# Adding the FFN's first bias on TensorE instead of ScalarE, and rectifying 512 columns at once

## The reference, cut to what matters

```
x_q  = fake_quant(layernorm(x), s1, -8, 7)
b1_q = fake_quant(b1, s1 * sw1, INT32_MIN, INT32_MAX)      # round(b1 / (s1*sw1)) * (s1*sw1)
h    = x_q @ W1_q.T + b1_q                                 # 256 -> 1024
h_q  = fake_quant(relu(h), s2, 0, 15)
out  = h_q @ W2_q.T + b2_q                                 # 1024 -> 256
```

## Time and profile before

| | |
|---|---|
| median of 3 runs | 298.29 us (298.26 to 298.51) |
| span of the profiled execution | 296.1 us |
| PE busy | 250.3 us (85% of the span) |
| DVE busy | 223.3 us (75%) |
| ACT busy | 202.2 us (68%) |
| POOL busy | 128.1 us (43%) |
| ACT `h_i` (L636), 128 operations | 48.3 us |

### The profile page before, as it was taken

The page is one execution under the profiler, slowest core; times in us unless marked ns, Lnnn a source line. Parts: engine busy times, 40 slices in busy tenths (PEclk is TensorE's granted clock), DMA queues, the critical chain, the costliest instruction groups (busy, mean ns, idle before and its releaser), DMA issues.

```text
span 296.1 us, 8723 instructions
## 1 busy us (share of the span) xinstructions
PE 250.3 (85%) x2816; PEld 183.8 (62%) x2816; DVE 223.3 (75%) x570; ACT 202.2 (68%) x444; POOL 128.1 (43%) x266
## 2 busy tenths in 40 slices
PE   0056227899999999999999999999999999999653
PEld 0045126867767777777777777777777767665441
DVE  2977418797887979797979797979888877784441
ACT  3213025667679787878787878888887978679423
POOL 7625039444471717263635454445453451520110
PEclk9999557799999999999999999999999999999875
DMA  7921101252111113121211121112112111200101
GB/s 165 340 92 45 35 0 38 62 167 49 37 48 45 45 45 83 41 52 41 80 45 45 40 80 43 45 51 68 44 38 72 41 38 41 72 3 4 35 0 38
DMA packets 31786, 17.41 MB, mean 59 GB/s; under 512 B 6544, under 2 KB 31376, under 8 KB 31760
## 3 DMA queue, kind: packets, MB, share of 16 engines
q1 hardware_dynamic: 29696, 17.06, 21.8%
q10 hardware_dynamic: 2064, 0.02, 0.4%
HBM read 6.31 MB, written 2.10 MB: 28 GB/s over the span
## 4 chain that ended last, share of the span: by engine, by line
PE 69%; issue 11%; DVE 10%; POOL 5%; ACT 4%; DMA 1%; ACTq 0%; POOLq 0%; DVEq 0%
PE ps_misc L972 34%; PE ps_av L972 13%; PE ps_max L972 12%; PE ps_exp L972 9%; DVE turns L697 2%; ACT h_i L636 2%; DVE xn L867 1%; DMA q_diag<-mxT 1%; POOL rot L475 1%; DVE by_cos L796 1%; POOL q_rows L441 1%; DVE by_sin L801 1%; DVE xn L772 1%; POOL k_rows L442 1%; POOL rstd L515 1%
## 5 line engine op out<-in xcount | busy, mean ns | idle before, releaser
L810 DVE TENSOR_REDUCE mx<-ps_max 128x4 f32<-128x512 f32 x128 | 87.3, 686 | 30.0 <-PE ps_max L972 26.9
L607 ACT ACTIVATE expo<-ps_exp 128x512 f32<-128x512 f32 x128 | 77.7, 607 | 19.6 <-PE ps_exp L972 18.1
L972 PE MATMUL ps_exp<-q_diag,k_stack 128*128 128x512 f32 x128 | 60.3, 471 | 0.4 <-DMA q_diag<-mxT 0.4
L972 PE MATMUL ps_av<-expo,v_strip 128*32 128x128 f32 x1024 | 54.1, 285 | 0.0
L972 PE MATMUL ps_max<-k_stack,q_diag 96*128 96x128 bf16 (+1 forms) x512 | 52.9, 226 | 0.8 <-DVE mx L810 0.8
L636 ACT ACTIVATE h_i<-ps_misc,b1q,relu_scale 128x128 int16<-128x128 f32 x128 | 48.3, 470 | 2.5 <-PE ps_misc L972 2.5
L972 PEld LDWEIGHTS ps_max<-k_stack,q_diag 96*128 96x128 bf16 (+1 forms) x512 | 30.8, 99 | 24.5 <-issue 23.3
L500 POOL TENSOR_TENSOR v_strip<-v_comp,zeros 128x32 f32<-128x32 f32 x128 | 28.0, 256 | 19.4 <-PE ps_av L972 19.4
L972 PEld LDWEIGHTS ps_av<-expo,v_strip 128*32 128x32 f32 x1024 | 20.3, 108 | 21.8 <-issue 14.7
L483 POOL TENSOR_TENSOR q_rows<-rot,q_rows 128x256 f32<-128x256 f32 x16 | 11.6, 725 | 36.0 <-ACT q_rows L582 36.0
L972 PEld LDWEIGHTS ps_exp<-q_diag,k_stack 128*128 128x128 f32 x128 | 24.4, 190 | 1.5 <-issue 0.8
(11 more groups left out here) (122 smaller groups left out, 514.3 us busy)
## 6 DMA issues: line engine op xcount, KB each, us to landing
q_diag<-q_comp SPq DMA_DIRECT2D x128, 64.0 KB, 2.0
w<-in_L_ffn_W_dram SPq DMA_DIRECT2D x2, 1024.0 KB, 8.2
out_dram<-y SPq DMA_DIRECT2D x8, 256.0 KB, 2.2
c_in<-in_ctx_dram SPq DMA_DIRECT2D x16, 64.0 KB, 2.1
x_all<-in_x_dram SPq DMA_DIRECT2D x1, 1024.0 KB, 5.8
x_all<-in_x_dram SPq DMA_DIRECT2D x1, 512.0 KB, 4.7
q_diag<-mxT SPq DMA_DIRECT2D x32, 8.0 KB, 1.8
x_all<-in_x_dram SPq DMA_DIRECT2D x2, 128.0 KB, 2.6
```

Of the source, the lines that this page charges most:

```text
L607: act.activation(expo[:, g % EXPO, :], ps_exp[g % 2][:, :], ACT.Exp, scale=SCALE).then_inc(exp_done, 1)
L810: dve.tensor_reduce(out=mx[:, r, 4 * g:4 * g + 4], in_=ps_max[g % 2][:, :].rearrange("p (h k) -> p h k", h=4), axis=AX.X, op=ALU.max).then ...
L972: return pe.matmul(out, lhsT, rhs, start=start, stop=stop, skip_group_check=True, **kw)
```

## The change

Two operations take the place of four per half. PE first writes the bias into the whole bank by one more product, 128 x 512, and the eight products of the half accumulate on it. Its weights are `b1_rows` (72 partitions x 128): the rounded b1, an integer, split into three bf16 parts whose sum is exact, at rows 0 to 7, 32 to 39 and 64 to 71, one row per block of 128 channels. The moving side is `b1_pick` (72 x 8 x 128), which holds ones where the row's block is the column's block. ACT then rectifies the half with one operation of 128 x 512 that keeps its scale from a pointer and has no bias.

What comes with it: b1 is loaded as 8 partitions x 128. POOL clears `b1_rows` and `b1_pick` in step 1, ahead of `v_strip`. ACT writes the ones into `b1_pick` by three copies in step 3 at g = 1. `round_b1` on DVE becomes eight operations on 8 x 128, six of them each waiting for the one before. PE waits once, at its first half, for both. `h_i` and `hq` now lie in the memory of the raw `w1`, which is not read any more by then.

```
@@ fill_strips (POOL, step 1)
+                pool.memset(b1_rows[:, :], 0.0).then_inc(b1_cleared, 1)
+                pool.memset(b1_pick[:, :, :], 0.0).then_inc(b1_cleared, 1)
+                pool.wait_ge(b1_cleared, 2)
                 pool.memset(v_strip[:, :, :, :], 0.0).then_inc(strips_ready, 1)
@@ relu (ACT)
-                for c in range(4):
-                    f = 4 * half + c
-                    ins = act.activation(h_i[:, r, f, :], ps_misc[PIECE_BANK[(H0, H1)[half]]][:, 128 * c:128 * c + 128],
-                                         ACT.Relu, bias=b1q[:, f:f + 1], scale=relu_scale[:, :])
-                ins.then_inc(relu_done, 1)
+                act.activation(h_i[:, r, 4 * half:4 * half + 4, :],
+                               ps_misc[PIECE_BANK[(H0, H1)[half]]][:, :].rearrange("p (f t) -> p f t", f=4),
+                               ACT.Relu, scale=relu_scale[:, :]).then_inc(relu_done, 1)
@@ body (ACT)
+                    if g == 1 and not st.looped and st.s == 3:
+                        act.wait_ge(b1_cleared, 2)
+                        for part in range(3):
+                            ones = bcast(ident[0:FC, 0:FC], 2, 128)
+                            act.copy(b1_pick[32 * part:32 * part + FC, :, :], ones).then_inc(b1_picked, 1)
@@ round_b1 (DVE)
-                link(dve.tensor_scalar(b1i[:, :], b1[:, :], r_h_scale[:, 0:1], None, ALU.mult), wprep)
-                dve.tensor_scalar(b1q[:, :], b1i[:, :], relu_scale[:, :], None, ALU.mult).then_inc(bias_ready, 1)
+                dve.wait_ge(b1_cleared, 2)
+                link(dve.tensor_scalar(b1i[:, :], b1[:, :], r_h_scale[0:FC, 0:1], None, ALU.mult), wprep)
+                link(dve.tensor_copy(b1f[:, 0, :], b1i[:, :]), wprep)
+                link(dve.tensor_copy(b1_rows[0:FC, :], b1f[:, 0, :]), wprep)
...
+                dve.tensor_copy(b1_rows[32:32 + FC, :], b1m[:, :])
+                dve.tensor_copy(b1_rows[64:64 + FC, :], b1f[:, 0, :]).then_inc(bias_ready, 1)
@@ hidden (PE)
+                if not st.looped and st.s == S_FFN and half == 0:
+                    pe.wait_ge(bias_ready, 2)
+                    pe.wait_ge(b1_picked, 3)
                 st.wait(pe, xqT_ready, S_FFN, 1, 1)
+                picked = b1_pick[:, 4 * half:4 * half + 4, :].rearrange("p f t -> p (f t)")
+                mm(ps[:, :], b1_rows[:, :], picked, True, False)
                 for f in range(4):
                     for c in range(DC):
                         ins = mm(ps[:, 128 * f:128 * f + 128], w1T[:, c, 4 * half + f, :],
-                                 xqT[:, r, 128 * c:128 * c + 128], c == 0, c == DC - 1)
+                                 xqT[:, r, 128 * c:128 * c + 128], False, c == DC - 1)
```

More of the change, by code:

```diff
@@ L22 @@
 QMIN, QMAX, HMAX = -8.0, 7.0, 15.0
+B1_ROWS = 2 * 32 + FC
 ROPE_FREQ = float(np.float32(10000.0) ** np.float32(-0.5))
@@ L161, in xattn_ffn_kernel @@
         b2q = sb("b2q", [128, DIM])
-        b1 = sb("b1", [128, FC])
-        b1i = sb("b1i", [128, FC], I32)
-        b1q = sb("b1q", [128, FC])
+        b1 = sb("b1", [FC, 128])
+        b1i = sb("b1i", [FC, 128], I32)
+        b1f = sb("b1f", [FC, 2, 128])
+        b1m = sb("b1m", [FC, 128], BF16)
+        b1_rows = sb("b1_rows", [B1_ROWS, 128], BF16)
+        b1_pick = sb("b1_pick", [B1_ROWS, FC, 128], BF16)
         w1 = sb("w1", [128, FC, DIM])
         w2 = sb("w2", [128, DC, FFN])
+        w_flat = [w1[:, :, :].rearrange("p c d -> p (c d)"), w2[:, :, :].rearrange("p c f -> p (c f)")]
         w_i = [sb("w1_i", [128, 2048], I16), sb("w2_i", [128, 2048], I16)]
@@ L228, in xattn_ffn_kernel @@
         xqT = sb("xqT", [128, 2, DIM], BF16)
-        h_i = sb("h_i", [128, 2, FC, 128], I16)
-        hq = sb("hq", [128, 2, FC, 128], BF16)
+        h_i = w_flat[0][:, 0:1024].bitcast(I16).rearrange("p (r f t) -> p r f t", r=2, f=FC)
+        hq = w_flat[0][:, 1024:2048].bitcast(BF16).rearrange("p (r f t) -> p r f t", r=2, f=FC)
         x2_b = sb("x2_b", [128, 2, DIM])
@@ L258, in xattn_ffn_kernel @@
         bias_ready = sem("bias_ready")
+        b1_cleared = sem("b1_cleared")
+        b1_picked = sem("b1_picked")
         wmax_ready = sem("wmax_ready")
@@ L330, in copy_wT @@
             copy(dst, src).then_inc(wT_ready[n % 2], 1)
-        w_flat = [w1[:, :, :].rearrange("p c d -> p (c d)"), w2[:, :, :].rearrange("p c f -> p (c f)")]
         out_pairs = out_d.rearrange("(k two) t d -> k t two d", two=2)
@@ L415, in _ @@
                 (wout[:, :, :], wout_d.rearrange("(c p) d -> p c d", p=128)),
-                (b1[:, :], b1_d.rearrange("(c p) -> p c", p=128)),
+                (b1[:, :], b1_d.rearrange("(c p) -> c p", p=128)),
                 (bout[:, :], all_rows(bout_d)),
@@ L631, in relu @@
                 st.wait(act, hq_ready, S_FFN, 2, half - 3)
-                if not st.looped and st.s == S_FFN and half == 0:
-                    act.wait_ge(bias_ready, 2)
-                for c in range(4):
-                    f = 4 * half + c
-                    ins = act.activation(h_i[:, r, f, :], ps_misc[PIECE_BANK[(H0, H1)[half]]][:, 128 * c:128 * c + 128],
-                                         ACT.Relu, bias=b1q[:, f:f + 1], scale=relu_scale[:, :])
-                ins.then_inc(relu_done, 1)
+                act.activation(h_i[:, r, 4 * half:4 * half + 4, :],
+                               ps_misc[PIECE_BANK[(H0, H1)[half]]][:, :].rearrange("p (f t) -> p f t", f=4),
+                               ACT.Relu, scale=relu_scale[:, :]).then_inc(relu_done, 1)
             def body(st):
@@ L748, in round_b1 @@
             def round_b1():
-                link(dve.tensor_scalar(b1i[:, :], b1[:, :], r_h_scale[:, 0:1], None, ALU.mult), wprep)
-                dve.tensor_scalar(b1q[:, :], b1i[:, :], relu_scale[:, :], None, ALU.mult).then_inc(bias_ready, 1)
+                dve.wait_ge(b1_cleared, 2)
+                link(dve.tensor_scalar(b1i[:, :], b1[:, :], r_h_scale[0:FC, 0:1], None, ALU.mult), wprep)
+                link(dve.tensor_copy(b1f[:, 0, :], b1i[:, :]), wprep)
+                link(dve.tensor_copy(b1_rows[0:FC, :], b1f[:, 0, :]), wprep)
+                link(dve.tensor_tensor(b1f[:, 1, :], b1f[:, 0, :], b1_rows[0:FC, :], ALU.subtract), wprep)
+                link(dve.tensor_copy(b1m[:, :], b1f[:, 1, :]), wprep)
+                link(dve.tensor_tensor(b1f[:, 0, :], b1f[:, 1, :], b1m[:, :], ALU.subtract), wprep)
+                dve.tensor_copy(b1_rows[32:32 + FC, :], b1m[:, :])
+                dve.tensor_copy(b1_rows[64:64 + FC, :], b1f[:, 0, :]).then_inc(bias_ready, 1)
             def norm1_stats(st):
```

## The result

The changed kernel takes 304.38 us, the median of 4 runs (303.50 to 305.47), against 298.40 us for the kernel before, the median of 4 runs (298.26 to 300.06). The ratio is 1.0199, with a 95% interval of 1.0157 to 1.0241: slower by 2.0%, clear of noise. The prediction had 303.5 us in a range of 301.0 to 305.2.

The account below looks back on a forecast made before the run. PE was taken to bound steps 6 to 18. Product 5.7, last steps -0.9 and filling +0.4 gave +5.2 us: span 296.1 to 301.3, median 298.29 to 303.5, range 301.0 to 305.2.

Parts of the forecast that it names:

- The bound and the product: Steps 6 to 18: PE sets the pace, nothing hides the added products, 13 x 2 x 0.22 = 5.7 us.
- Rival A: Steps 6 to 18: the product is half hidden and costs 0.13 us, so +2.9, 301.2 us; chance 0.09.
- The rectifier: ACT, each half: one operation of 0.70 us replaces four of 1.50 together; worth time only in the last three steps.
- The last steps: Steps 19 to 21: shorter rectifier less added products gives -0.9 us, ends -0.3 and -2.7.
- Step 20: Second-to-last step: sooner rectified first half less the late second half, together -0.22 us at the half clock.
- Its first term: Step 20, up to PE's transposes: product in front and short rectifier, 0.22 - 0.80 = -0.58 us.
- The second: Step 20, second half: its added product takes 0.43 us at the half clock, of which about 0.36 stick out.
- the branch with the full clock: Step 20: if PE's clock stays full because the gap before it shrinks, the step gives -1.4 us.
- Rival C: From 268 us on: all PE gaps go and the clock stays full, 7.2 us gained, 298.1 us; chance 0.03.
- The filling steps: Before step 6: POOL's clears cost 0.4 us; ACT's copies, DVE's chain, b1's DMA and moved buffers cost 0.
- rival B: Steps 4 and 5: DVE's chain delays maxima and their DMA, PE's clock falls; +7.4, 305.7 us; chance 0.07.
- a first full step over 1 us late: Start of the first full step: beginning over 1 us late would show the forecast wrong and point to rival B.

Follow-up runs that it names:

- one rectifier alone: Kernel before with one 128 x 512 rectifier per half, the bias left out, no product and no preparation; 295.01 us, ratio 0.9889.
- no product: Changed kernel without the bias product, so b1 is left out of the result; preparation and single rectifier stay; 295.97 us, ratio 0.9933.
- two products: Changed kernel with the bias product issued twice per half, the second writing the same values again; 310.06 us, ratio 1.038.
- the end on DVE: Kernel before with the first half in bank 2 from step 18, and DVE doing ACT's four operations per half in steps 20 and 21; 298.40 us.
- another bank: Kernel before with the first half of the hidden layer in bank 2 from step 18 on, no operation changed; 296.28 us, ratio 0.9931.
- the preparation alone: Changed kernel's whole preparation in its places, but four rectifiers per half with raw b1 as bias and no product; 299.88 us, ratio 1.0043.
- the chain spread: Changed kernel with DVE's eight `round_b1` operations one per group in step 5 instead of in a row in step 4; 304.17 us, ratio 1.0167.
- the end alone in another bank: Kernel before, with early-issued product and single rectifier only in steps 20 and 21, first half in bank 2 from step 18, preparation moved earlier; 294.98 us.
- the version prepared late: As the end alone in another bank, but clears in step 16, DVE's rounding in step 17, ACT's copies in steps 17 to 19; 296.88 us.

## Why the prediction was right, point by point

**The bound and the product: right.** The prediction read PE as busy throughout in steps 6 to 18 and priced 26 products at 0.22 us, 5.7. The trace shows 5.78, and the steps of 14.45, 14.89 and 15.325 us with none, one and two products show that nothing hides any part of it. Rival A (a half hidden) is out. The Trainium skill, "TensorE: Matmul & The Clock Gate", section "Back-to-back issue gap", gives about 131 ns for a product of 512 columns in a sustained stream and 216 for an isolated one. In this busy stream it was 220, which agrees with the second figure and not with the first; the measurement decides.

**The rectifier: right in size.** Chosen 0.70 us, measured 0.687. That it is worth nothing where PE doesn't wait for it is shown by the kernel with one rectifier alone. The Trainium skill, "ScalarE: Activation LUTs", section "What ACT_TABLE_LOAD costs", gives 706 ns by its formula; the trace has 687, within 3% of it.

**The last steps: mechanism right, one term mis-sized.** Predicted -0.9, in the trace -2.16. Step 19 (-0.04 predicted, -0.11 measured) and step 21 (-0.5, -0.43) came out. Step 20 gave -1.62 where the sum had -0.22. Its first term was right: from the start of the half to the transposes it is 1.61 us instead of 2.20, -0.59 where the prediction had -0.58. The second was not: from there to the next first half it is 6.82 instead of 7.85, -1.03 where the prediction had +0.36 at the half clock. The clock was full there, and the branch with the full clock (-1.4 for the step) is what came. Rival C needed the full clock in step 21 as well, and there it was half.

That a shorter gap brings the full clock is likely, but no rule. Over the 3.1 us from the transposes of step 20 on, the mean clock is 0.50 and 0.63 in the two traces with the gap of 1.60 us. With the gap of 0.78 it is 1.00 in six traces, but 0.54 and 0.52 in those of no product and two products. With a gap of 0.37 it is 1.00 for the end on DVE and 0.51 for another bank.

**The filling steps: mis-sized the other way.** Predicted +0.4, in the trace +1.88, by the medians of the preparation alone +1.2. What failed is the step from POOL's clears to the maxima. Their own part, 0.45 at `rstd`, was as predicted (0.4), but the issue time ahead of the maxima is no constant: 5.59 to 5.93 us in the five kernels that clear nothing in the filling steps, 5.62 to 6.41 in the nine that do. In the trace of the preparation alone `rstd` is 0.48 us late (27.09), the maxima 0.88, step 6 0.56. For the DVE chain, which I then suspected, the run with the chain spread shows no gain. ACT's copies were not run by themselves. The first trace has PE waiting 0.97 us for ACT's `q_comp` at 52.00, behind them, but the transpose that waited 1.47 for DVE at 52.43 comes at 53.52, 1.09 late, no more than the maxima. How the rest divides stays open.

By its own sign, a first full step over 1 us late, the forecast had to yield to rival B in the first trace. What B said is not in it: PE has no wait for the DMA in step 4 there, and the clock is full from 60 us on. In the second execution of the changed kernel even the sign is absent. But B's picture does occur. The two latest starts of step 6, 91.77 (no product) and 90.20 (chain spread), follow waits for that DMA of 1.63 and 1.20 us, behind which the mean clock is 0.50 and 0.70 up to 70 us. Behind one of 1.47 (the end alone in another bank) it stayed at 1.00. Over all traces step 6 begins at 87.18 to 88.01 us in the five kernels without clears in the filling steps, at 87.42 to 91.77 in the six that clear in step 1, and at 88.46 to 89.30 in the three that clear in step 0.

**The sum.** +5.2 predicted; +5.5 in the trace, as 5.78 + 1.88 - 2.16; +4.7 to +6.0 by medians. Two errors, of about 1.3 in the end and of 0.8 to 1.5 in the filling, had opposite signs and nearly cancelled. That the total was good to 1 us was partly luck.

## What to carry to other kernels

Moving work to relieve an engine costs its full price on the engine that sets the pace, and gains only where that engine waits: here 13 steps paid 0.44 us each for a gain that the last steps alone could use. Do such a thing only in those steps, and first ask whether the wait can be removed without any operation, by giving the piece another buffer. Before placing preparation on an engine that is idle half of the time, look at what stands directly behind it: if that is the head of a chain, its idle time hides little. And look at what the other engines run beside it.

## What the runs showed of the hardware

- POOL's fill is priced by the element of a partition, not by the byte: 1024 bf16 columns took 0.94 us, 2048 f32 columns 1.81, 4096 int32 columns 3.51.
- DVE and POOL do not meet at semaphores alone. An operation of DVE of 128 x 64 (`turns`), which waits for nothing of POOL's, took 4.65 us instead of 0.20 and ended 0.06 us behind POOL's fill of `q_diag`; with 1.0 us more of fills behind that it took 5.68. Other operations of DVE ran beside fills at their usual length, such as `wmax` over 2048 columns, 2.27 us beside the fills of step 1 (at 24.05 in the changed kernel) and 2.28 with none beside it (at 20.45).
- A wait of PE can be paid twice. In the version prepared late a wait of 2.06 us was followed by a step at a mean granted clock of 0.90 that took 13.32 instead of 12.21 us. At the end, a gap of 0.78 instead of 1.60 was followed by the full clock in six traces and by about half of it in two, so a single trace doesn't settle what a gap costs.
- The clock in the filling steps and the issue time ahead of the shared maxima change from one execution to the next: the same 17 us at 0.50 in one and at 1.00 in another, 6.36 against 5.76 us. A difference of 1 us read there from one pair of traces is no finding; it needs medians.
